# AdaLN block with a selective scan and a mixture of experts: a third buffer for the state, sums begun last in GpSimd's slot, and neighbouring work moved between slots

## The reference, cut to what matters

```python
# x: (4, 2048, 512); six rows of 512 for each batch (sa, ca, ga, sb, cb, gb) come from silu(c) @ wmod
h = layernorm(x) * (1 + ca) + sa
x = x + ga * mamba(h)
h = layernorm(x) * (1 + cb) + sb
x = x + gb * ffn(h)

# mamba(h), 16 states for each of 512 channels
val, gate = split(h @ W_in);  val = silu(conv3(val))
B, C  = val @ W_B, val @ W_C
Delta = softplus((val @ W_delta + delta_base) @ W_tau);  dA = Delta * A
A_bar = exp(dA);  B_bar = expm1(dA) / (dA + 1e-6) * Delta * B
for t in range(2048):                        # lax.scan, for every channel and state
    s = A_bar[t] * s + B_bar[t] * val[t];  y[t] = sum over states of s * C[t]
out = (y * silu(gate)) @ W_out + h

# ffn(h): 8 experts, the best 2 of each token by sigmoid(h @ gate_W), and a shared one; hidden width 256
sum over experts of gate * (gelu(h @ W1 + b1) @ W2 + b2)
```

## Time and profile before

| | us |
|---|---|
| runs | 5478.98, 5497.39, 5493.48; median 5493.48 |
| profiled execution | 5478.18 |
| its span, first to last instruction | 5476.4 |
| busy: VectorE | 4403.8 (80%) |
| busy: ScalarE | 4051.8 (74%) |
| busy: TensorE | 4017.3 (73%) |
| busy: GpSimd | 3658.4 (67%) |
| mean busy share of the 16 DMA engines in scan 0 to 511 | 0.71 |

### The profile page before, as it was taken

The page is one execution under the profiler, slowest core; times in us unless marked ns, Lnnn a source line. Parts: engine busy times, 40 slices in busy tenths (PEclk is TensorE's granted clock), DMA queues, the critical chain, the costliest instruction groups (busy, mean ns, idle before and its releaser), DMA issues.

```text
span 5476.4 us, 36465 instructions
## 1 busy us (share of the span) xinstructions
PE 4017.3 (73%) x9708; PEld 1675.1 (31%) x9708; DVE 4403.8 (80%) x3862; ACT 4051.8 (74%) x4199; POOL 3658.4 (67%) x2132
## 2 busy tenths in 40 slices
PE   7531415787787878787888888787877875959889
PEld 3210102233333333333333333333333332323343
DVE  1388799989898898989888889989898989889210
ACT  2586777888888887888888887888888877878111
POOL 0299876677777776777777777676777777777211
PEclk8765657898888898898889898898889896979889
DMA  4487867677676767677677767676676666677322
GB/s 137 152 256 226 250 154 208 174 212 197 194 206 198 209 181 229 169 218 192 193 210 199 204 190 214 175 219 191 185 214 199 194 181 188 181 201 187 122 92 73
DMA packets 338776, 1037.14 MB, mean 189 GB/s; under 512 B 40197, under 2 KB 43141, under 8 KB 331270
## 3 DMA queue, kind: packets, MB, share of 16 engines
q1 hardware_dynamic: 274058, 799.91, 44.3%
q0 software_dynamic: 64512, 234.91, 22.0%
HBM read 673.29 MB, written 126.51 MB: 146 GB/s over the span
## 4 chain that ended last, share of the span: by engine, by line
DMA 23%; issue 19%; PE 17%; DVE 16%; ACT 12%; POOL 11%; POOLq 0%; SPq 0%; DVEq 0%; ACTq 0%
DMA ysum<-hs 22%; POOL hs L1282 6%; PE ps L1023 6%; DVE ps L1077 3%; DVE ps L1084 3%; PE ps L1039 3%; PE ps L993 3%; DVE ps L1071 3%; ACT inv L675 2%; POOL hid L1310 2%; DVE xa L1144 2%; POOL inv L1298 1%; ACT th L682 1%; DVE ps L1091 1%; PE ps L984 1%
## 5 line engine op out<-in xcount | busy, mean ns | idle before, releaser
L1298 POOL TENSOR_TENSOR inv<-inv,th 128x1024 f32<-128x1024 f32 x512 | 1331.2, 2600 | 275.3 <-ACT th L682 275.2
L1282 POOL TENSOR_TENSOR hs<-hs,Cb 128x1024 f32<-128x1024 f32 x512 | 1249.7, 2441 | 262.9 <-DVE hs L1104 227.6
L1039 PE MATMUL ps<-w2r,hid 128*128 128x512 f32 x2304 | 1142.9, 651 | 19.8 <-DVE x L1130 19.7
L1023 PE MATMUL ps<-hf,w1r 128*128 128x512 f32 x2304 | 1131.0, 646 | 2.9 <-DMA w1r<-in_W 2.3
L1050 PE MATMUL ps<-Brow,pick 48*128 48x512 bf16 x1024 | 362.3, 439 | 997.3 <-DVE hs L1104 996.7
L670 ACT ACTIVATE inv<-nrd,kappa 128x1024 f32<-128x1024 f32 x512 | 557.4, 1140 | 383.0 <-DVE ps L1084 379.0
L682 ACT ACTIVATE th<-delta,halfA 128x1024 f32<-128x1024 f32 x512 | 582.7, 1138 | 279.3 <-POOL inv L1298 279.3
L1104 DVE TENSOR_TENSOR_SCAN hs<-abar,ps 128x1024 f32<-128x1024 f32 x256 | 583.5, 2279 | 234.2 <-DMA ysum<-hs 231.1
L1291 POOL DMA_DIRECT2D ysum<-hs x448 | 391.9, 875 | 509.9 <-issue 399.8
L1104 DVE TENSOR_TENSOR_SCAN hs<-abar,carry,ps 128x1024 f32<-128x1024 f32 x256 | 598.7, 2338 | 158.5 <-DMA ysum<-hs 158.3
L1071 DVE TENSOR_TENSOR ps<-ps,us 128x1024 f32<-128x1024 f32 x512 | 627.5, 1226 | 79.0 <-PE ps L1050 41.7
(11 more groups left out here) (150 smaller groups left out, 4870.2 us busy)
## 6 DMA issues: line engine op xcount, KB each, us to landing
Cb<-c_rows SPq DMA_DIRECT2D x512, 512.0 KB, 4.9
ysum<-hs POOLq DMA_DIRECT2D x448, 512.0 KB, 6.6
w2r<-w_scaled SPq DMA_DIRECT2D x144, 512.0 KB, 8.0
w1r<-in_W SPq DMA_DIRECT2D x144, 512.0 KB, 4.3
gbc<-expert_gates SPq DMA_DIRECT2D x128, 256.0 KB, 3.7
aw<-in_W_val SPq DMA_DIRECT2D x64, 256.0 KB, 7.9
xa<-in_x SPq DMA_DIRECT2D x16, 1024.0 KB, 8.5
h_residual<-hT SPq DMA_DIRECT2D x16, 1024.0 KB, 11.1
```

Of the source, the lines that this page charges most:

```text
L1023: mm = t.matmul(o, w1r[:, n % 2, k, h * P:(h + 1) * P], hf[:, k, :], start=(k == 0), stop=(k == G - 1))
L1039: mm = t.matmul(o, hid[:, e % HB, h, tt * P:(tt + 1) * P], w2r[:, e % 3, h, :], start=(grp < 2 and e % 3 == 0 and h == 0), stop=(e % 3 == ...
L1282: gp_.tensor_tensor(hs[:, c % 2, :], hs[:, c % 2, :], Cb[:, c % 2, :], ALU.mult).then_inc(hC_done, 1)
L1298: gp_.tensor_tensor(inv[:, c % 6, :], inv[:, c % 6, :], th[:, c % 2, :], ALU.mult).then_inc(thinv_done, 1)
```

## The change

- `hs` has three buffers instead of two, and the scan of state c waits for the sum of state c - 3.
- In GpSimd's slot, times_C comes first, then the extra work, then `weight`, and last the sum (`add_to_y`, split off from times_C).
- `us` has two buffers; its load goes out in slots 8 and 24.
- The room for this is taken from `hid`: four tiles instead of six, the hidden tiles of places 3 and 4 lie in `xn` (`hidden`).
- Statistics of x1: tile 0 in slot 6, tiles 1 and 2 in slot 7, tile 3 and the aggregation early in slot 8, instead of all late in slot 8; the square root at ScalarE's w = 2 "start" instead of "half logs"; the reciprocals late in slots 9 and 25 instead of early in 10 and 26.
- ScalarE: take_t2 ahead of softplus_exp(0); the sigmoid at w = 3 "squared" instead of place 0; take_w1(4) and (5) one place earlier; the normalizing of xa at w = 6 "squared" instead of place 1; take_t at w = 6 place 3 and w = 7 "start", ahead of the gelu.
- VectorE copies the B/C product in slot 13 instead of 12, and SyncE stores C's rows in slot 13.
- TensorE: the w1 jobs 2 to 7 move back by up to one slot, the transposes t from slots 28 and 29 to 27 and 28; the planner's due times follow.

```diff
-        us = sb("us", [P, TB])
+        us = sb("us", [P, 2, TB])
-        hs = sb("hs", [P, 2, TB])
+        hs = sb("hs", [P, 3, TB])
-        hid = sb("hid", [P, HB, HT, T])
+        hid = sb("hid", [P, HB - 2, HT, T])
+        def hidden(p):
+            i = p % HB
+            return xn[:, 2 * (i - 3):2 * (i - 3) + 2, :] if i in (3, 4) else hid[:, i if i < 3 else 3]
...
-            if r in (14, 30) and 0 <= c // N + 1 < NU:
+            if r in (8, 24) and 0 <= c // N + 1 < NU:
...
-                ge(sp, uB_done, N * u)
-                sp.dma_start(us[:], u_d[u // G, u % G]).then_inc(us_ld, 16)
+                ge(sp, uB_done, N * (u - 1))
+                sp.dma_start(us[:, u % 2, :], u_d[u // G, u % G]).then_inc(us_ld[u % 2], 16)
...
-            if r == 12:
+            if r == 13:
                 if has(qa):
                     sp.wait_ge(ev_bc, qa + 1)
                     sp.dma_start(c_d[qa // 2, :, half], bct[N:2 * N, :]).then_inc(st_c, 16)
...
-                    if place == "half logs" and has(qf):
+                    if place == "start" and has(qf):
                         act.wait_ge(f_stat, (TPB + 1) * (qf + 1))
                         s.activation(rstdF[:, :, 0], momF[:, :, 1], ACT.Sqrt, bias=consts[:, 0:1]).then_inc(f_sqrt, 1)
...
                     if place == 2:
+                        take_t2(qf, (0, 1))
+                    if place == 3:
+                        take_t2(qf, (2, 3))
                         softplus_exp(qa, 0)
-                    if place == 3:
-                        take_t2(qf, (0, 1))
                 if w == 3:
                     if place == "start":
-                        take_t2(qf, (2, 3))
                         softplus_exp(qa, 1)
...
-                    if place == 0 and has(qf):
+                    if place == "squared" and has(qf):
                         act.wait_ge(mm_log, qf + 1)
...
+                    if place == 2:
+                        take_w1(qf, 4)
                     if place == 3:
-                        take_w1(qf, 4)
+                        take_w1(qf, 5)
                 if w == 5:
-                    if place == "start":
-                        take_w1(qf, 5)
...
-                    if place == 1 and has(qn):
+                    if place == "squared" and has(qn):
                         act.wait_ge(a_rstd, 2 * qn + 2)
...
+                    if place == 3:
+                        take_t(qn, (0, 1))
                 if w == 7:
                     if place == "start":
+                        take_t(qn, (2, 3))
                         gelu(qf, 2)
-                    if place == "squared":
-                        take_t(qn, (0, 1))
-                    if place == "half logs":
-                        take_t(qn, (2, 3))
...
-                13: [("log", qf, 0), ("w1", qf, 0)], 14: [("w1", qf, 1), ("w1", qf, 2)],
-                15: [("gT", qf, 0), ("w1", qf, 3), ("w1", qf, 4)], 16: [("w1", qf, 5), ("w1", qf, 6)],
-                17: [("w1", qf, 7)], 18: [("w1", qf, 8), ("w1", qf, 9)], 19: [("w1", qf, 10)],
+                13: [("log", qf, 0), ("w1", qf, 0)], 14: [("w1", qf, 1)],
+                15: [("w1", qf, 2), ("gT", qf, 0), ("w1", qf, 3)], 16: [("w1", qf, 4), ("w1", qf, 5)],
+                17: [("w1", qf, 6), ("w1", qf, 7)], 18: [("w1", qf, 8), ("w1", qf, 9)], 19: [("w1", qf, 10)],
...
-                27: [("w2", qf, 4)], 28: [("w2", qf, 5), ("t", qn, 0), ("t", qn, 1)], 29: [("w2", qf, 6), ("t", qn, 2), ("t", qn, 3)],
+                27: [("t", qn, 0), ("t", qn, 1), ("w2", qf, 4)], 28: [("w2", qf, 5), ("t", qn, 2), ("t", qn, 3)], 29: [("w2", qf, 6)],
...
-                    if c >= 2:
-                        if (c - 2) % N < 2:
-                            dve.wait_ge(y_begun, unit(c - 2) + 1)
+                    if c >= 3:
+                        if (c - 3) % N < 2:
+                            dve.wait_ge(y_begun, unit(c - 3) + 1)
                         else:
-                            dve.wait_ge(y_summed, 16 * sums(c - 2))
+                            dve.wait_ge(y_summed, 16 * sums(c - 3))
...
-                if r == 8 and has(qf):
-                    dve.wait_ge(ev_out, TPB * (qf + 1))
-                    stats_of(x1, statsF, momF, f_stat, qf * (TPB + 1))
-                if r == 12 and has(qa):
+                if r in (6, 7) and has(qf):
+                    dve.wait_ge(ev_out, TPB * qf + (1 if r == 6 else 3))
+                    tile_stats(x1, statsF, f_stat, (0,) if r == 6 else (1, 2))
+                if r == 13 and has(qa):
...
-                    gp_.tensor_tensor(hs[:, c % 2, :], hs[:, c % 2, :], Cb[:, c % 2, :], ALU.mult).then_inc(hC_done, 1)
-                    if c % N:
-                        pool.wait_ge(hC_done, c + 1)
+                    gp_.tensor_tensor(hs[:, c % 3, :], hs[:, c % 3, :], Cb[:, c % 2, :], ALU.mult).then_inc(hC_done, 1)
+
+            def add_to_y(c):
+                if 0 <= c < NC and c % N:
+                    u = unit(c)
+                    pool.wait_ge(hC_done, c + 1)
+                    if c % N == 1:
+                        ge(pool, y_gated, u)
+                        gp_.tensor_tensor(ysum[:], hs[:, (c - 1) % 3, :], hs[:, c % 3, :], ALU.add).then_inc(y_begun, 1)
+                    else:
                         ge(pool, y_summed, 16 * sums(c - 1) if c % N > 2 else 0)
...
+                        pool.wait_ge(y_begun, u + 1)
+                        gp_.dma_start(ysum[:], hs[:, c % 3, :], accum_op=ALU.add).then_inc(y_summed, 16)
...
             times_C(c - 1)
-            weight(c + 2)
...
+
+            weight(c + 2)
+            add_to_y(c - 1)
```

More of the change, by code:

```diff
@@ L760, in take_w1 @@
                         act.wait_ge(mm_w1, HT * (EX * q + e) + h + 1)
-                        s.activation(hid[:, e % HB, h, :], ps[:, bank_of["w1", q, HT * e + h], :], ACT.Identity,
+                        s.activation(hidden(e)[:, h, :], ps[:, bank_of["w1", q, HT * e + h], :], ACT.Identity,
                                      bias=b1_sb[:, EXPERTS[e] * HT + h:EXPERTS[e] * HT + h + 1]).then_inc(ev_w1, 1)
@@ L767, in gelu @@
                     for e in GROUPS[grp]:
-                        s.activation(hid[:, e % HB], hid[:, e % HB], ACT.Gelu).then_inc(gelu_done, 1)
+                        s.activation(hidden(e), hidden(e), ACT.Gelu).then_inc(gelu_done, 1)
             def inverse_delta(u, place):
@@ L905, in bank_held_to @@
                 return at + 1.95
-            held = {"t": (29, 29, 30, 30), "val": (1.5, 2.5, 3.5, 3.9), "gate": (8.3, 8.4, 9.5, 9.6), "p": (10.9, 11, 11.4, 11.5),
-                    "bc": (14,), "t2": (12, 12.1, 12.6, 12.7), "log": (14.95,), "gT": (15.9,),
-                    "w1": (14.4, 14.5, 15.4, 15.5, 16.5, 16.6, 18, 18.1, 19.3, 19.4, 20.9, 21, 25.3, 25.4, 25.8, 25.9,
-                           26.5, 26.6)}[kind]
+            held = {"t": (28.7, 28.7, 29.5, 29.5), "val": (1.5, 2.5, 3.5, 3.9), "gate": (8.3, 8.4, 9.5, 9.6), "p": (10.9, 11, 11.4, 11.5),
+                    "bc": (14.6,), "t2": (12, 12.1, 12.6, 12.7), "log": (14.95,), "gT": (15.9,),
+                    "w1": (15.4, 15.5, 15.9, 16.3, 17, 17.2, 19.4, 19.5, 20.6, 20.7, 21, 21.1, 25.1, 25.2, 25.8, 25.9,
+                           27.4, 27.5)}[kind]
             return start + held[i]
@@ L1038, in job @@
                         for h in range(HT):
-                            mm = t.matmul(o, hid[:, e % HB, h, tt * P:(tt + 1) * P], w2r[:, e % 3, h, :],
+                            mm = t.matmul(o, hidden(e)[:, h, tt * P:(tt + 1) * P], w2r[:, e % 3, h, :],
                                           start=(grp < 2 and e % 3 == 0 and h == 0), stop=(e % 3 == 2 and h == HT - 1))
@@ L1097, in scan, with tile_stats, mean_and_variance @@
                     dve.wait_ge(bu_done, c + 1)
-                    if c >= 2:
-                        if (c - 2) % N < 2:
-                            dve.wait_ge(y_begun, unit(c - 2) + 1)
+                    if c >= 3:
+                        if (c - 3) % N < 2:
+                            dve.wait_ge(y_begun, unit(c - 3) + 1)
                         else:
-                            dve.wait_ge(y_summed, 16 * sums(c - 2))
+                            dve.wait_ge(y_summed, 16 * sums(c - 3))
                     first = (u // G) % (L // TB) == 0
-                    v.tensor_tensor_scan(hs[:, c % 2, :], abar[:, c % 4, :], X(c),
+                    v.tensor_tensor_scan(hs[:, c % 3, :], abar[:, c % 4, :], X(c),
                                          0.0 if first else carry[:, u % G, c % N:c % N + 1], ALU.mult, ALU.add).then_inc(scan_done, 1)
-            def stats_of(src, st, mom, sm, base_):
-                for tt in range(TPB):
+            def tile_stats(src, st, sm, tts):
+                for tt in tts:
                     v.bn_stats(st[:, tt, :], src[:, tt, :]).then_inc(sm, 1)
+            def mean_and_variance(st, mom, sm, base_):
                 dve.wait_ge(sm, base_ + TPB)
@@ L1209, in early @@
```

(27 more changed lines are left out.)

19 lines of the change are left out of this document (7 added, 12 removed).

## The result

The changed kernel takes 5220.19 us (median of 4 runs, 5219.21 to 5228.76), the kernel before on the same chips 5487.01 (4 runs): ratio 0.9516, 95% interval 0.9494 to 0.9538. That is 267 us less, where 203 was forecast and 5290 us; 5220 lies near the lower edge of the forecast's own range, 5215 to 5365.

The account below looks back on a forecast made before the run. VectorE, busy 268.7 of 304.4 us a window, was taken as the bound, losing time waiting for sums. Savings of 8 + 6 + 1 + 1 - 2 = 14 us over 14.5 windows, 203 us, gave 5290 us; range 5090 to 5450.

Parts of the forecast that it names:

- The likeliest case: Whole kernel: 14 us a window saved, 5290 us, chance 0.52, its own range 5215 to 5365 us.
- Slots 8 to 15, 8 saved: VectorE's waits in slots 8 to 15: of 11.7 us a window some 4 stay, 8 saved.
- Slots 22 to 31, 6 saved, 12 left: VectorE's 18 us idle there: 3 for GpSimd, 5 from late normalizing and 4 for serial sums stay, 6 saved.
- The slow serial sums: Sums from 27 on stay serial beside loads: 2 us at scan 30 and 2 at the window's edge.
- the 3 us for GpSimd as the bound: Slots 22 to 31: GpSimd needs 82 us, VectorE 79, so 3 us stay even with no buffer wait.
- Elsewhere 1 and u 1: Waits in slots 0, 6 and 21: 1 of 3 us saved; VectorE's wait of 1.0 us for u goes.
- Covers that fail, 2 lost: Moved statistics, W1 jobs and other steps may lack slack beside other work: 2 us a window lost, from nothing to 5.
- Landing as before, 6.6 us: A sum's DMA was taken from the trace: 6.6 us to landing in the median, 4.5 at the least.
- nearly all waits go: Rival: later sums meet fewer loads, land in 4.5 to 6 us, never hold a scan; 5085 to 5145 us, chance 0.12.
- VectorE's work unchanged: Same instructions after the moves, so VectorE's busy time per window stays within 5 us.
- a collision risk of either sign: VectorE's softplus instructions meeting GpSimd's in SBUF: 5.4 us a window lost or 7.1 won, +78 or -103 us.
- GpSimd's wait for tanh shorter: GpSimd does extra work while it stood for tanh (6.21 us in slot 10), so that wait shrinks.

Follow-up runs that it names:

- The moves alone: The changed kernel with two buffers of h, the old order on GpSimd and one buffer of u: 5525.72 us, ratio 1.0077 to the kernel before.
- The last run: Product for rstd made by four one-element instructions instead of one, in the kernel with xa's normalizing moved back (5149.31 us): 5142.52 us, ratio 0.9381.

## Why the prediction was right, and where its terms were off

The likeliest case held in its time and its outline: nearly all waits for sums go, and some of the time comes back as waits for other engines. Part of that was luck. The buffer was priced at nearly all of 24.3 us a window and alone gave 75 us in the run; the later issue was priced mostly as a cost, 2.6 to 5.6 us of the 7.8 paid back, and beside the buffer the new order gave 144. Two steps that were wrong in opposite directions left the sum near the truth. From the scans of states 96 and 448 a window takes 288.0 us for 306.3, 18.3 less, and 18.3 times the 14.5 windows of the forecast is 265 of the 267 us. The 14 us a window were the term that was too small. In window 8, by its own steps:

- *Slots 8 to 15, 8 saved*: 9.1. The waits of 1.7 and 1.3 for sums 9 and 10, worked out with landings of 9.4 and 8.6 us, didn't come; 2.4 us of what is left is a wait for ScalarE's xa in the softplus.
- *Slots 22 to 31, 6 saved, 12 left*: 6.5 and 11.7, but by other parts. The late normalizing was seen with its size in the mean (with it moved back a window takes 283.1 us for 288.0, 5 less; forecast 5), not its path. It went through abar (3.4) and TensorE's bank for `take_w1(8)` (5.3), not through weight 28 and the sum behind it: the weight is waited for 0.2 us. The slow serial sums came to 2.3 for 4, and the 3 us for GpSimd as the bound show in no wait.
- *Elsewhere 1 and u 1*: 2.6. *Covers that fail, 2 lost*: none beside the one of slot 27 in this window's waits; of the 4 us a window that were missed this is the largest part.
- *Landing as before, 6.6 us*: the step that failed in substance. I priced the later issue as 2.6 us lost and never looked at what starts beside the issue. In the trace of before, SyncE issued a load of C at 2794.82, 0.28 ahead of the sum at 2795.10. There 258 of the 448 sums start less than 0.8 us behind a load of C and land in 7.0 us in the median, the others in 5.9. In the changed kernel 6 do, and sums land in 5.1. This is the reason that I had given to the rival "nearly all waits go", and the runs with the sum at once and with C's load later show it. The scan's wait came out at 59.6, not 100 to 200; how much of that is due to the landings isn't shown, as no run has three buffers, the late issue and landings of 6.6 us, and with the early issue and 6.6 us the scan waits 67.0 and 15.2. The prediction called itself wrong if landings changed by over 1 us in the median: they changed by 1.5.
- *VectorE's work unchanged*: 268.46 for 268.70, but not for the reason given. In the whole run its softplus subtraction (L1144 before) takes 67.8 us for 102.0, and the products for rstd 73.1 for 52.8. The moves alone add 48 us to the kernel before, and the old order kept in the changed kernel adds 54 to that one; the sum issued last took that back. So 54 of the 144 us of the order stand in this column, which I had called a collision risk of either sign.
- *GpSimd's wait for tanh shorter*: wrong, 386.6 for 275.2, while its wait at the issue fell by 170.6. Two things feed it: with the normalizing moved back it is 312.9, 74 less, and with the old order 260.4, 126 less. That the wait at the issue turned into the wait for tanh isn't shown: with C's load later, against the sum at once, the first fell by 222 us and the second rose by 49.
- *Windows of about 291 us*: 286.0 in window 8, 288.0 in the mean.

The estimate of 3.2 us for such a DMA (the Trainium skill, DMA: Bandwidth & Descriptors, Anatomy of one DMA) was met by no landing of a sum: the shortest was 4.4. But 1.5 us of the 6.6 were not the DMA's own, and leaning on the median of a trace in which more than half of the sums start together with a load hid that.

What stays open: how much of the 54 to 85 us of VectorE's busy time that come with an early sum would be won if they alone went. The last run says that such time can come back as waits. No run has the third buffer and the late issue without the moves, so what the moves are worth in the changed order isn't known either.

**To carry to other kernels.** When an issue is moved, look in the timeline for what else is released by the same event: a transfer that starts 0.3 us ahead cost more here than the delay did. A wait of 389 us that goes uncovers those behind it, so a buffer and the moves that feed it must be priced together: alone they changed the time by -75 and +44 us, with the second u and the late sums by -267. And with waits at 8 us in 283, 51 us of work taken from the fullest engine gave 7 us here.

## What the runs showed of the hardware

- A 512 KB transfer from SBUF to SBUF, adding, that started less than 0.8 us behind a 512 KB load from DRAM landed in 7.0 us in the median (258 of the kernel before), the load in 4.5. By whole runs the adding one takes 6.6 us where its issue stands right behind the product (4 runs and the kernel before) and 5.0 to 5.5 where it comes later or the load does.
- A VectorE instruction with two SBUF operands can take far longer than the one GpSimd instruction that it meets. L1125, 0.16 us at the least, took 8.69 us: it began under L1339 and ended at 2535.93, with L1342 (2535.90), the fourth from there. The Trainium skill (SBUF — State Buffer, Who interferes with whom) has the loser blocked for the other's whole length; here it lost to four in a row, with a DMA issue among them. In the kernel before L1144 (1.22 us at the least) takes 5.15 where it lies over two in a row, so the prediction's "the trace agrees" holds for the blocking and not for its length.
- The form with one SBUF tensor and a scalar per partition took 0.20 to 0.22 us in all 128 cases of one element. That doesn't carry over to every instruction with one SBUF tensor: L1145, a TENSOR_SCALAR over 128x1024 with two constants, took 0.70 us in the median and 2.73 at the most in the changed kernel, and 7.69 with the sum at once behind the product, again under GpSimd instructions without a gap. The Trainium skill (SBUF — State Buffer, Who interferes with whom) has an instruction with at most one SBUF input free of this contention outside the performance modes that use two ports; no run here shows which mode L1145 was in.
